# Bias rows written by ScalarE, lookups on 32 rows of the array and a new order ahead of the loop, in a fused attention and embedding kernel

## What is computed

```python
# layer 0: modulated linear, attention over 16 heads inside a token, modulated linear
style = s @ aff_w.T + aff_b
w_mod = w[None] * style[:, None, :]
w_mod = w_mod * rsqrt(sum(w_mod * w_mod, axis=2) + eps)
modulated_linear = einsum('bni,boi->bno', x, w_mod) + b      # kx: b is k_b; out: b is o_b
scores = einsum('bnhd,bnjd->bnhj', kx, kx) / sqrt(32)        # 16 x 16 scores of each token
out = einsum('bnhj,bnjd->bnhd', softmax(scores), kx)
x = x + modulated_linear(out)
# layer 1: layer norms with gains and offsets looked up by token ids, then a two layer MLP with a norm
h = _ln(_ln(x, pw_g[pathway_ids], pw_b[pathway_ids]), cp_g[compartment_ids], cp_b[compartment_ids])
t = _ln(x, tm_g[time_steps], tm_b[time_steps])
s = _ln(x, ms_g[scale_type], ms_b[scale_type])
m, n, r = x + a vector of the batch each (small MLPs of the states, layer norm)
cat = concatenate([w[0]*h, w[1]*t, w[2]*m, w[3]*n, w[4]*r, w[5]*s])
x = x + _ln(silu(cat @ int_W1 + int_b1) @ int_W2 + int_b2, int_g, int_be)
```

## Time and profile before

| | |
|---|---|
| median of three runs | 938.13 us |
| the profiled execution, its time | 936.79 us |
| its span in the trace | 935.0 us |
| mean granted clock of TensorE | 0.968 |
| TensorE busy | 876.8 us, 94% |
| VectorE busy | 698.0 us, 75% |
| GpSimd busy | 592.5 us, 63% |
| ScalarE busy | 450.6 us, 48% |
| DMA | 93.78 MB, mean 100 GB/s |

### The profile page before, as it was taken

One profiled execution on the slowest core, in us unless ns is written; L12 is line 12 of the kernel. 1 busy time (PEld: TensorE's weight loads), 2 busy tenths in 40 slices (PEclk: granted clock), 3 DMA queues, 4 the chain that ended last, 5 costly groups with the idle time before them and its releaser, 6 DMA issues.

```text
span 935.0 us, 19902 instructions
## 1 busy us (share of the span) xinstructions
PE 876.8 (94%) x7518; PEld 789.8 (84%) x7566; DVE 698.0 (75%) x1129; ACT 450.6 (48%) x790; POOL 592.5 (63%) x742
## 2 busy tenths in 40 slices
PE   5876798999999999999999999999999999999987
PEld 5744697988989898998989898998979898999886
DVE  3679867778697777778787777778787777768642
ACT  3565336454544546454544645454544645453421
POOL 2267797766566675756576675856676675857551
PEclk9987799999999999999999999999999999999999
DMA  8951232422333232323334242323334242222110
GB/s 291 414 203 33 70 97 69 119 56 93 97 110 111 81 108 68 108 54 104 99 91 130 69 119 69 90 50 116 102 84 122 68 117 64 93 53 85 35 46 23
DMA packets 101871, 93.78 MB, mean 100 GB/s; under 512 B 72720, under 2 KB 75024, under 8 KB 100112
## 3 DMA queue, kind: packets, MB, share of 16 engines
q1 hardware_dynamic: 91984, 67.93, 24.0%
q0 software_dynamic: 4608, 16.78, 6.5%
q10 hardware_dynamic: 5184, 7.79, 2.7%
HBM read 67.83 MB, written 8.39 MB: 82 GB/s over the span
## 4 chain that ended last, share of the span: by engine, by line
PE 50%; DVE 26%; issue 9%; ACT 7%; another core or an unknown queue 4%; POOL 2%; DMA 2%; ACTq 1%; DVEq 0%; SPq 0%; POOLq 0%
PE acc L368 30%; PE tok L368 12%; PE att L368 3%; PE xp L511 3%; PE xp L368 2%; DVE norm L1280 2%; DVE ytmp L1266 2%; DVE SE L1195 2%; DVE small L1199 1%; DVE SE L1222 1%; DVE SE L1210 1%; DMA p_kb<-in_kb 1%; ACT pgb L795 1%; DVE alo L1228 1%
## 5 line engine op out<-in xcount | busy, mean ns | idle before, releaser
L1476 POOL TENSOR_TENSOR xlo<-xraw,xhi 128x512 fp32r<-128x512 f32 x32 | 46.8, 1464 | 104.8 <-ACT xhi L736 104.8
L1530 POOL TENSOR_TENSOR op1l<-ytmp,op1h 128x512 fp32r<-128x512 f32 x64 | 84.2, 1316 | 31.1 <-ACT op1h L824 30.7
L368 PE MATMUL acc<-op1h,W1th 128*128 128x256 f32 x256 | 80.2, 313 | 10.9 <-POOL op1l L1530 10.9
L368 PE MATMUL acc<-op0h,W1xh 128*128 128x256 f32 x256 | 77.2, 301 | 1.5 <-DVE op0l L1252 1.5
L824 ACT CAST op1h<-ytmp 128x512 fp32r<-128x512 f32 x64 | 39.7, 621 | 78.6 <-DVE ytmp L1266 78.6
L368 PE MATMUL acc<-op1h,W1hh 128*128 128x256 f32 x256 | 77.5, 303 | 0.0
L368 PE MATMUL acc<-op1l,W1th 128*128 128x256 f32 x256 | 77.4, 302 | 0.0
L368 PE MATMUL acc<-op1h,W1tl 128*128 128x256 f32 x256 | 77.3, 302 | 0.0
L368 PE MATMUL acc<-op0h,W1sh 128*128 128x256 f32 x256 | 73.7, 288 | 0.0
L368 PE MATMUL acc<-op0h,W1xl 128*128 128x256 f32 x256 | 73.0, 285 | 0.0
L368 PE MATMUL acc<-op0l,W1xh 128*128 128x256 f32 x256 | 73.0, 285 | 0.0
(11 more groups left out here) (248 smaller groups left out, 3201.2 us busy)
## 6 DMA issues: line engine op xcount, KB each, us to landing
xsq<-in_x SPq DMA_DIRECT2D x32, 256.0 KB, 4.3
xb<-in_x SPq DMA_DIRECT2D x32, 256.0 KB, 2.9
out<-xb SPq DMA_DIRECT2D x32, 256.0 KB, 2.0
xraw<-in_xT SPq DMA_DIRECT2D x31, 256.0 KB, 4.3
BD<-q SPq DMA_DIRECT2D x124, 64.0 KB, 2.1
BD<-v SPq DMA_DIRECT2D x124, 64.0 KB
ring<-in_k_wT ACTq DMA_DIRECT2D x12, 256.0 KB
ring<-in_o_wT ACTq DMA_DIRECT2D x12, 256.0 KB
```

Of the source, the lines that this page charges most:

```text
L368: return e.matmul(o, a, b, start=start, stop=True, skip_group_check=True)
L1476: e.tensor_tensor(xlo[:, :, :], xraw[:, :, :], xhi[:, :, :].bitcast(F32), ALU.subtract).then_inc(s["xlo"], 1)
L1530: e.tensor_tensor(op[slot]["l"][:, :, half(g)], four(ytmp[YT[n, g][0]]), op[slot]["h"][:, :, half(g)].bitcast(F32), ALU.subtract).then_inc ...
```

## The change

TensorE: the matmul with selT behind proj stays for the odd tiles and for tiles 0 and 2 and goes for the even tiles from 4 on; that behind W2 goes everywhere. ScalarE writes the bias (k_b or int_b2, broadcast over the partitions in SBUF) into the bank ahead of the matmuls, which then accumulate onto it. Odd tiles but the last are copied by ScalarE from tok1 to a ytmp tile when W2 is done; the last norm reads the copy, and proj waits for the copy instead of the norm. The lookups use 32 partitions of `tab` and OH, the tables GT go, and lookup s(pb) moves behind the last W1 t part, next to h(pa). VectorE: product(pb, t) ahead of mod_lo; the norm is cut in two, last_stats and last_gain; last_gain(pb) goes behind x_one(b), or into the next iteration where that has no mod_lo. Ahead of the loop the order changes, three table rows are made by ScalarE from PSUM, split3(1) goes into iteration 1, and some DMAs change places.

```diff
@@ build @@
-        selT = at("selT", [128, 2, 128], BF16)
+        selT = at("selT", [128, 128], BF16)
-        GT = {n: at("G" + n, [128, 512], BF16) for n in "tsh"}
+        kb = at("kb", [128, 512])
+        b2 = at("b2", [128, 512])
-            return {...  "vT": (s["vT"], 1),
+            return {...  "vT": (s["LB"], 6),
+        def copied(g):
+            return g % 2 == 1 and g < NG - 1
@@ sync @@
-            e.dma_start(rp[:, :], A["rows_p"]).then_inc(s["c_rv"], 16)
...
-            e.wait_ge(s["hn"], 1)
-            e.dma_start(gint[:, :], A["int_g"].partition_broadcast(128)).then_inc(s["c_gi"], 16)
+            e.wait_ge(s["stt"], 8)
+            e.dma_start(rp[:, :], A["rows_p"]).then_inc(s["c_rp"], 16)
+            load_tok(2)
+            load_tok(3)
             for k in range(1, NT + 1):
...
-                if k == 1:
-                    e.wait_ge(s["pT"], 1)
-                    load_tok(2)
-                    load_tok(3)
...
                 if front:
                     blocks_v(b)
+                if k == 1:
+                    e.wait_ge(s["pT"], 1)
+                    e.dma_start(gint[:, :], A["int_g"].partition_broadcast(128)).then_inc(s["c_gi"], 16)
@@ tensor @@
             def proj(g, kts=range(4)):
+                on_bias = g > 3 and g % 2 == 0
...
+                    elif on_bias:
+                        e.wait_ge(s["sd"], g // 2 - 1)
+                    elif g > 3:
+                        e.wait_ge(s["wc"], g // 2 - 1)
...
-                    three(..., kt == 0)
+                    i = three(..., kt == 0 and not on_bias)
                 if kts[-1] == 3:
-                    mm(o[:, :], selT[:, 0, :], tab[:, :]).then_inc(s["A"], 1)
+                    if not on_bias:
+                        i = mm(o[:, :], selT[:, :], tab[:, :])
+                    i.then_inc(s["A"], 1)
             def gains(g, n):
+                q = quad({"t": 0, "s": 1, "h": 3}[n])
                 for c in range(4):
-                    i = mm(..., GT[n][:, c * 128:c * 128 + 128], OH[(g // 2) % 2][:, half(g)], start=(c == 0))
+                    i = mm(..., tab[q, c * 128:c * 128 + 128], OH[(g // 2) % 2][q, half(g)], start=(c == 0))
             def W2_part(g, ms):
+                if ms[0] == 0:
+                    e.wait_ge(s["sw"], g + 1)
...
-                    three(..., m == 0)
+                    i = three(..., False)
+                if ms[-1] == 3:
+                    i.then_inc(s["W2"], 1)
-            def W2_last(g):
-                W2_part(g, (2, 3))
-                mm(tok[g % 2][:, :], selT[:, 1, :], tab[:, :]).then_inc(s["W2"], 1)
...
+            values(1)
             vec_T()
-            values(1)
             z_T(0)
+            a_T(1)
             tables_mnr()
-            a_T(1)
...
                     a_T(a)
+                W1_part(k - 1, "t", 1, (1,))
+                if front:
                     gains(pb, "s")
-                W1_part(k - 1, "t", 1, (1,))
                 gains(pa, "h")
@@ scalar @@
+            def bias_q(g):
+                e.wait_ge(s["ql"], g)
+                e.copy(tok[1][:, :], kb[:, :]).then_inc(s["sd"], 1)
+            def bias_2(g):
+                if g % 2 == 0:
+                    e.wait_ge(s["x1"], min(g + 3, NG))
+                elif g < NG - 1:
+                    e.wait_ge(s["ql"], min(g + 4, NG))
+                else:
+                    e.wait_ge(s["w"], NG - 2)
+                e.copy(tok[g % 2][:, :], b2[:, :]).then_inc(s["sw"], 1)
+            def w_copy(g):
+                y = take_y(e, ("w", g))
+                e.wait_ge(s["W2"], g + 1)
+                e.copy(y[:, :], tok[1][:, :]).then_inc(s["wc"], 1)
...
+            e.dma_start(b2[:, :], A["b2"].partition_broadcast(128)).then_inc(s["c_ob"], 16)
...
-            e.copy(vT[...], xp[...]).then_inc(s["vT"], 1)
+            for i, n in enumerate("mnr"):
+                j = e.activation(L[n][...], four(xp[...])[...], ACT.Copy, scale=w7[:, 2 + i:3 + i])
+                j.then_inc(s["LB"], 1)
...
                     e_first(a)
+                if k > 1:
+                    z_copy(pb)
                 if mod:
                     mod_hi(*mod, (0, 1))
-                if k > 1:
-                    z_copy(pb)
                 prod_hi(pb, "t")
...
                 u_make(pb)
+                if k == 1:
+                    e.wait_ge(s["tA"], 2)
+                    e.copy(t2[:, 256:512].bitcast(BF16), rp[:, :]).then_inc(s["tp"], 1)
...
                     prod_hi(pb, "s")
+                    if more:
+                        bias_q(a + 2)
                 prod_hi(pa, "h")
...
                     z_make(a)
+                    bias_2(pa)
                     sum_part(b, "S", "Sc")
                     if more:
                         q_hi(a + 2)
                     exponential(b)
+                    bias_2(pb)
...
                         sum_part(a + 2, "S", "Sc")
+                    w_copy(pb)
+                    if more:
                         exponential(a + 2)
                     x1_hi(a)
@@ vector @@
-            def gain_tables():
...
-            vectors_end()
-            x_one(0)
-            e_T(1)
+            vectors_norm()
+            e_T(1)
+            x_one(0)
+            e_second(1)
+            vectors_end()
             q_lo(2)
-            e_second(1)
-            for n in "mnr":
-                table_rows(n)
+            a_sum(1)
             q_T(2)
-            x_weights(1, range(4))
-            a_sum(1)
-            x_weights(2, (0, 1))
+            x_weights(1, (0, 1))
             a_lo(1)
-            x_weights(2, (2, 3))
-            v_stats(0)
+            x_weights(1, (2, 3))
+            x_weights(2, range(4))
             product(0, "t")
             v_T(2)
+            v_stats(0)
+            x_one(1)
+            x1_lo(0)
             split_lo(W1["x", "l"], ...)
-            x_one(1)
-            x1_lo(0)
...
-            split3(1, rp[:, :], PT[:, :])
+            late = False
             for k in range(1, NT + 1):
...
+                product(pb, "t")
                 if mod:
                     mod_lo(*mod, (0, 1))
-                product(pb, "t")
+                if late:
+                    last_gain(pb - 2)
                 if k > 1:
                     finish(pb - 2)
...
                     q_T(b)
+                    if k == 1:
+                        split3(1, rp[:, :], PT[:, :])
                     a_lo(a)
...
-                last_norm(pa)
+                last_stats(pa)
+                last_gain(pa)
...
-                last_norm(pb)
+                last_stats(pb)
                 if front:
                     x_one(b)
+                late = front and not mod_of(k + 1)
+                if not late:
+                    last_gain(pb)
+                if front:
                     x1_lo(a)
@@ gpsimd @@
             true_scale(0)
+            demod(0, 1)
+            demod(1, 1)
...
-                if k < 3:
-                    demod(k - 1, 1)
```

145 lines of the change are left out of this document (70 added, 75 removed).

## The result

The changed kernel takes 933.53 us (median of 20 runs, 931.43 to 937.61) against 937.30 us for the kernel before (20 runs): a ratio of 0.9973, 95% interval [0.9962, 0.9984]. That is 2.5 us less by the ratio and 3.8 by the medians, a small gain whose interval just leaves out no change, where 915 us with a range of 896 to 930 and a chance of 0.93 for faster had been forecast. The profiled execution took 931.67 us, its span 929.9 us, 5.1 us less than before. (The span's ends vary from one execution to the next: the first out_proj starts between 60.2 and 62.4 us, and the stretch behind the last one differs by up to 2 us.

What follows compares the result with a forecast made beforehand. TensorE, busy 94% of the span, and its waits were taken as the bound. The terms summed as 936.8 - 10.6 - 3.7 - 18.1 + 16.8 - 6.0 = 915.2, say 915 us, range 896 to 930 us.

Steps and rivals of the forecast that it cites:

- What bounds the kernel: Whole span: TensorE busy 94%, VectorE 75%, ScalarE 48%, so time is won on TensorE's work or waits.
- Part 1: Bias rows behind W2 and in even tiles 4 to 30: dropping 46 selT matmuls at 0.23 us saves 10.6 us.
- part 2: Odd tiles at proj(b): ScalarE's copy frees the tok1 bank earlier, saving 15 x 0.25 = 3.7 us.
- Part 3: Six long iterations: t product ahead of the low parts closes a hole and restores the clock, net 18.1 us saved.
- The hole of 1.71 us: TensorE's idle time behind a long iteration's attention matmuls: closes, and with it goes the lower clock costing 1.7 us.
- a_lo ... ends by 227.7: Long iteration, VectorE: q_T(b) ends at 227.0, then a_lo takes 0.67 us; TensorE would arrive at 227.3.
- The give-back: out_proj(a) late behind a_lo in the six long iterations: 0.4 us each, 2.4 us in all.
- the hole stays in another place: Rival, 13%: a_lo or op1l late, or the clock falls anyway; 2.5 us lost per long iteration, 930 us.
- Part 4: Lookups with 32 rows: entering and leaving cost 0.22 us for each of 80 groups, less overlap, +16.8 us.
- Part 5: Ahead of the loop: moving split3 and reordering brings out_proj(2) to about 116 us, saving 6 us; bounds nothing to 10.
- the walk of the queues: Start, up to out_proj(2): queues followed with today's durations put it at about 116 us, 6 us saved.

Runs made afterwards that it cites:

- e_alo: Changed kernel with VectorE's two weight copies of blocks 2 and 3 moved behind a_lo(a): 933.6 us, ratio 0.9951 to the kernel before.
- Part 3 alone: Kernel before with only the t product ahead of the new weights' low parts and the z copy ahead of their high parts: 931.4 us, ratio 0.9929.
- e_gt: Changed kernel with 128-row lookups from gain tables again, and the 14 even tiles' selT matmuls back: 925.9 us, ratio 0.9875 to the kernel before.
- e_k32: Kernel before with only the t, s and h lookups changed to read 32 rows of the plain table: 949.7 us, ratio 1.0123.
- e_s3l: Changed kernel with split3 of the table rows moved behind the h product of the first iteration: 928.2 us, ratio 0.9911 to the kernel before.
- e_w1s: Changed kernel with GpSimd's split of W1's s block moved behind the second gather: 930.0 us, ratio 0.9919 to the kernel before.
- e_dve: Changed kernel with three of GpSimd's low-part splits of the integrator weights made by VectorE: 929.6 us, ratio 0.9933 to the kernel before.
- e_nolo: Changed kernel with VectorE's low parts of new weight blocks 0 and 1 made for 8 of 512 columns: 923.8 us, ratio 0.9873 to the kernel before.

## Why the prediction failed, step by step

**What bounds the kernel: half right.** "Time is won by taking work from TensorE, or by removing waits of TensorE" holds for the plain iterations, which came out at 50.78 us against 50.9. For the long ones it was the wrong reading of a share: VectorE is busy 75% of the span, but in the changed kernel 10.00 of 10.00 us in the stretch of a long iteration around a_lo. The kernel before had 1.1 to 2.4 us of idle time of VectorE ahead of a_lo there, and the change used it up.

**Part 1 (10.6 us) and part 2 (3.7 us): right in the plain iterations, too large elsewhere.** The copies are on ScalarE at 0.58 us, and no matmul of the changed kernel waits for one. The 46 matmuls alone brought 8.0 us [5.3, 10.6], some of it luck of the clock, and the rest needs part 2. In the long iterations, which hold 18 of the 46, they free an engine that then waits. Part 2 had VectorE's reads move to SBUF at the same count; the gain operation on the copy, both of whose inputs are now in SBUF, took 1.19 us instead of 0.75 in 8 of its 15 places; the plain iterations, in which such places lie, show no wait of TensorE over 0.2 us.

**Part 3 (18.1 us): this step failed.** The hole of 1.71 us closed and the clock came back, as forecast, and TensorE's arrival was nearly right: 7.84 us from its attention matmuls to the h lookup (221.49 to 229.33), which is 8.16 to out_proj(a), against 7.83.

What failed is "a_lo ... ends by 227.7", in two ways. First, the product stands 2.0 us later in this execution than forecast (219.19 against 217.20, since this stretch began 2.1 us later), so on its scale that is 229.7; a_lo ended at 231.1. The durations of mod_lo and mod_weights were taken over from a trace in which GpSimd stood beside the first low part alone; in the new order GpSimd's op1l runs beside the second, and in iterations 3 and 12 its add_ob beside mod_weights. They took 1.6 us more in these two and 0.5 us in the other four, by an estimate (2 x 1.6 + 4 x 0.5) 5.2 of the 6.6 us of the six waits.

Second, a_lo also waits for ScalarE's ahi, which the forecast left out: in the kernel before a_lo started at 229.42 and not at 227.0, 2.43 us of idle time behind q_T(b), and in e_alo, where VectorE is early, ahi alone keeps TensorE 0.5 us at a_lo. The give-back put down at 0.4 us was 1.83 us at a_lo in two iterations and 0.73 to 0.77 in four, and four of the six had another 0.4 us behind it, at the new weights or at the product.

Part 3 alone brought 6.6 us of the 18.1. The wait went from GpSimd's low part to a_lo, which is the rival *the hole stays in another place* (13%, 930 us) by its mechanism. That its 930 us are near the measured time is luck: the long iterations missed by 1.6 us each and not by 2.5, and the 7.0 us of part 5 made up the sum.

**Part 4 (16.8 us): the price right, the count wrong.** 0.21 us a group net of the overlap (e_gt), 0.25 in e_k32. But it was charged 80 times, and in the long iterations it costs nothing: VectorE is late anyway. In e_k32 it even closed part of the hole, and in five of six iterations the clock stayed up. Between 5 and 12 us remain. The Trainium skill (TensorEngine Tiling (Array Packing), Key Properties) says that changing the mode drains the engine; the runs agree and put the price at 0.09 us entering and 0.12 leaving, with 0.03 at the matmul behind. The sign of this part was right: without it the change would be worth 12 us (e_gt) instead of 2.5.

**Part 5 (6.0 us): this step failed too.** Its lower bound was "nothing, since split3 now stands ahead of a_lo(2)", and this is what happened, and worse: A is 1.6 us longer. out_proj(2) came 60.2 us behind out_proj(0) instead of the 55.4 that 6.0 us less would be (61.4 before). Two things failed in the walk of the queues. It gave too little to the order: split3, no slower than before, holds a_lo(2) for 4.53 us, and e_s3l, which moves it away, brings out_proj(2) 5.1 us forward. And it took the weight sums ahead of v_stats(0) at durations that they did not keep: the eight of this stretch took 11.1 us instead of 8.8, and with GpSimd's split away from four of them (e_w1s) the wait at u_T(0) is 2.66 us instead of 5.70.

A large share of the failures is one: **VectorE's time was read as a property of its operations, and it is also one of what GpSimd does beside them.** The Trainium skill says so (SBUF — State Buffer, SBUF: two separate sides): VectorE and GpSimd share a pair of ports as an exclusive lock, which counts for VectorE's operations with two inputs in SBUF and for those in a two-port mode. The rows agree with its form: the operations that are longer beside GpSimd (a low part of the weights 1.2 to 1.8 us instead of 0.68, split3's second subtraction 1.77 instead of 0.69, the weight sums 1.45 instead of 0.7) have both inputs in SBUF, and a_lo and the products, with one input in PSUM, took 0.65 to 0.70 us wherever they stood, a_lo(2) at 119.88 beside an operation of GpSimd among them. (split3's scaling, with one input only, grew as well: 1.51 us at 113.42, 0.48 in e_dve.) It can fall on either engine: in iteration 4 mod_weights kept 0.75 us an operation and GpSimd's add_ob took 1.59 us instead of 1.29. The kernel before had shown it: mod_lo's 2.38 us for two are nearly twice the 1.28 of the two at 230.03, and GpSimd's affine stood beside the first.

What stays open: where the 2.8 us between out_proj(2) and out_proj(4) come from, beyond the wait of 2.27 us for e; and how much of the 2.3 us that two long iterations and the one behind keep in e_nolo (4.1 less 1.8 for mod_rows) is VectorE's and how much the chain of the weights. And the splits of GpSimd inside A were tried in two places each only.

## What to carry to other kernels

Read an engine's busy share from the stretch in which the change acts, not from the span: where another engine is full there, neither a gain nor a cost on TensorE is seen. When a move brings two engines' work side by side that had stood one behind the other, price both again; for VectorE beside GpSimd, an operation with two SBUF inputs took up to 1.8 us here instead of 0.7, or waited out a row of GpSimd's (4.47 us). A sum of durations is also not enough where the operation waits for a third engine: look in the trace before for what ended its idle time. Before work is handed to another engine's queue, look for who issues the DMA that depends on it, and what stands behind that issue.
